# Sixteen-head attention: the value product in four passes with both halves of v in one stationary tile, its parts summed off TensorE, and the next rows normalized one slot earlier

## The reference

```
def _attention(x, W_qkv, W_out, b_out):
    qkv = x @ W_qkv                                   # 256 -> 3 x 1024
    q, k, v = jnp.split(qkv, 3, axis=-1)              # 16 heads of 64 each
    attn = jnp.einsum('bqhd,bkhd->bhqk', q, k) * DH ** (-0.5)
    attn = jax.nn.softmax(attn, axis=-1)
    out = jnp.einsum('bhqk,bkhd->bqhd', attn, v).reshape(Bq, Tq, INNER)
    return out @ W_out + b_out
x = x + g_msa * _attention(_modulate(_layernorm(x), sh_msa, sc_msa), W_qkv, W_out, b_out)
```

## Time and profile before

| | |
|---|---|
| median of 3 runs (1896.93 to 1900.22) | 1899.54 us |
| the profiled execution: its time, its span | 1899.73 us, 1897.6 us |
| share of the span busy: PE, PEld, DVE, ACT, POOL | 92%, 84%, 71%, 60%, 46% |
| granted TensorE clock, mean | 0.966 |
| the sixteen-head attention | about 262 to 1120 us |
| TensorE, idle before an instruction of the attention, from 300 to 1100 us | 27.7 us |

### The profile page before, as it was taken

One profiled execution on the slowest core, in us unless ns is written; L12 is line 12 of the kernel. 1 busy time (PEld: TensorE's weight loads), 2 busy tenths in 40 slices (PEclk: granted clock), 3 DMA queues, 4 the chain that ended last, 5 costly groups with the idle time before them and its releaser, 6 DMA issues.

```text
span 1897.6 us, 36653 instructions
## 1 busy us (share of the span) xinstructions
PE 1754.8 (92%) x12739; PEld 1587.3 (84%) x12739; DVE 1355.4 (71%) x3357; ACT 1146.9 (60%) x2858; POOL 873.6 (46%) x949
## 2 busy tenths in 40 slices
PE   5888979999999999999999979999888989989998
PEld 3657878888889888888889979999777978879997
DVE  5878866676777767677677665555999969985663
ACT  3445646666666666666666655556655746656664
POOL 1535645655665555656565533332444523331111
PEclk7999989999999999999999989999999989989999
DMA  8222200000000000000000001110111112220111
GB/s 288 64 56 70 87 20 4 10 10 10 10 10 10 9 8 10 4 10 10 10 10 10 7 15 31 29 30 27 47 43 50 52 25 44 46 58 23 45 45 45
DMA packets 110969, 65.87 MB, mean 35 GB/s; under 512 B 81530, under 2 KB 92788, under 8 KB 110788
## 3 DMA queue, kind: packets, MB, share of 16 engines
q1 hardware_dynamic: 110788, 63.54, 12.3%
HBM read 59.06 MB, written 4.46 MB: 33 GB/s over the span
## 4 chain that ended last, share of the span: by engine, by line
PE 77%; DVE 10%; issue 6%; ACT 5%; POOL 1%; DMA 1%; DVEq 0%; POOLq 0%; SPq 0%; ACTq 0%
PE bank L255 21%; PE bank L257 20%; PE bank L256 20%; PE bank L1036 7%; PE bank L985 6%; PE bank L379 2%; DVE xn L342 2%; DVE hl L577 1%; PE bank L438 1%; ACT nf L392 1%; DVE nTlo L399 1%; DVE aTlo L399 1%; ACT nThi L392 1%; ACT prob L1008 1%; DVE upd L608 1%
## 5 line engine op out<-in xcount | busy, mean ns | idle before, releaser
L1023 POOL TENSOR_SCALAR prob<-prob,rinv 128x256 f32<-128x256 f32 x512 | 467.3, 925 | 343.0 <-DVE rinv L1017 342.1
L571 ACT ACTIVATE hf<-bank,vecs 128x512 f32<-128x512 f32 x240 | 168.0, 700 | 302.4 <-PE bank L257 302.4
L577 DVE TENSOR_TENSOR hl<-hf,hh 128x512 fp32r<-128x512 f32 x240 | 196.7, 820 | 157.4 <-ACT hh L571 157.0
L1045 ACT ACTIVATE pthi<-bank 128x512 fp32r<-128x512 f32 x272 | 164.6, 605 | 196.5 <-PE bank L1036 193.9
L1008 ACT ACTIVATE prob<-bank,nmax 128x256 f32<-128x256 f32 x544 | 253.8, 479 | 39.6 <-DVE nmax L1281 21.1
L998 DVE TENSOR_REDUCE nmax<-bank 128x2 f32<-128x512 f32 x256 | 175.6, 686 | 142.1 <-PE bank L985 141.8
L334 POOL TENSOR_TENSOR rstd<-vareps,mhalf 128x2 f32<-128x2 f32 x128 | 106.1, 829 | 343.9 <-DVE vareps L330 343.2
L257 PE MATMUL bank<-WBhi,hh 128*128 128x256 f32 x768 | 217.7, 284 | 0.0
L256 PE MATMUL bank<-WBlo,hh 128*128 128x256 f32 x768 | 217.6, 283 | 0.0
L255 PE MATMUL bank<-WBhi,hl 128*128 128x256 f32 x768 | 217.3, 283 | 0.0
L255 PE MATMUL bank<-aThi,WAlo 128*128 128x256 f32 x576 | 177.4, 308 | 41.1 <-DVE aTlo L399 31.7
(11 more groups left out here) (164 smaller groups left out, 5310.6 us busy)
## 6 DMA issues: line engine op xcount, KB each, us to landing
gates<-gate_scratch SPq DMA_DIRECT2D x96, 256.0 KB, 3.7
agate<-gate_scratch SPq DMA_DIRECT2D x32, 256.0 KB, 3.2
stage<-in_L_cond_W SPq DMA_DIRECT2D x64, 64.0 KB, 2.3
out<-x SPq DMA_DIRECT2D x16, 256.0 KB, 2.2
adaw<-in_L_cond_Wc SPq DMA_DIRECT2D x1, 3072.0 KB, 17.9
stage<-in_L_cond_W_qkv SPq DMA_DIRECT2D x8, 384.0 KB, 3.5
x<-in_x SPq DMA_DIRECT2D x1, 2560.0 KB, 16.8
stage<-in_L_cond_ff_w SPq DMA_DIRECT2D x32, 64.0 KB, 2.1
```

Source lines behind the costliest of these rows:

```text
L571: last = act.activation(dst[:, :], U_BANKS[c % 2][:, :], ACTF[p], bias=vecs[:, at:at + 1])
L577: dve.tensor_tensor(hl[r][:, :], hf[r][:, :], hh[r][:, :].bitcast(F32), ALU.subtract).then_inc(h_lo, 1)
L1023: last = pool.tensor_scalar(dst[:, q, :], dst[:, q, :], rinv[i][:, q:q + 1], None, ALU.mult)
L1045: act.activation(pt[i][0][:, :], PTB[i][:, :], ACT.Copy).then_inc(pt_hi, 1)
```

## The change

Each head now has 128 columns of one tile `vv`: an even head its 64 rounded columns and then its 64 low ones, an odd head its low ones first. One pass with that stationary tile gives both products at once, the one with the rounded half in 64 partitions and the one with the low half in the other 64. Four passes a head are left (two blocks of keys, each with the low and the rounded half of the probabilities), and every head has its own 256 columns of OB. The zeros and their memsets go. The sum of the two parts is now made by other engines: ScalarE copies the low part of each head into the partitions of the main part (`oc`, two instructions a pair), VectorE adds (`of`, two instructions a pair, `o_add`) and rounds (`o_round`), and GpSimd makes the remainder (`o_rest`). TensorE's next pair waits for the two additions (`o_sum`). The copies of v from PSUM are one instruction for two. The next rows' transposes are issued in slot 9 for slot 10, the first two of their four ScalarE instructions in slot 9, the others in slot 10 ahead of the exponential, and their normalization by VectorE in slot 6 for slot 8.

```diff
-        VP = 3 * DH
-        vv = [sb(f"v{k}", [P, TPB, PAIRS * VP], F32R, att) for k in ("hi", "lo")]
+        VP = 4 * DH
+        vv = sb("vv", [P, TPB, PAIRS * VP], F32R, att)
+        of = [sb(f"of{i}", [P, SEQ], scope=att) for i in range(2)]
+        oc = sb("oc", [P, SEQ], scope=att)
...
             if h % 2 == 0 and H:
-                pe.wait_ge(o_lo, H // 2)
-            i, at = h // 2 % 2, h // 2 * VP + h % 2 * DH
+                pe.wait_ge(o_sum, H)
             for c in range(TPB):
-                last = split3(pe, OB[:, i * SEQ:(i + 1) * SEQ], [m[:, c, at:at + P] for m in vv],
-                              [m[:, c * SEQ:(c + 1) * SEQ] for m in pt[h % 2]],
-                              c == 0 and h % 2 == 0, c == TPB - 1 and h % 2 == 1)
+                for m in (1, 0):
+                    last = pe.matmul(OB[:, h % 2 * SEQ:(h % 2 + 1) * SEQ], vv[:, c, h * P:(h + 1) * P],
+                                     pt[h % 2][m][:, c * SEQ:(c + 1) * SEQ],
+                                     start=c == 0 and m == 1, stop=c == TPB - 1 and m == 0, skip_group_check=True)
             last.then_inc(pv_mm, 1)
 
-        def o_read(act, pair, i):
+        def o_halves(j):
+
+            main, rest = slice(j * DH, (j + 1) * DH), slice((1 - j) * DH, (2 - j) * DH)
+            return main, rest, slice(j * SEQ, (j + 1) * SEQ)
+
+        def o_read(act, pair):
 
             act.wait_ge(pv_mm, 2 * pair + 2)
+            if pair:
+                act.wait_ge(o_sum, 2 * pair)
+            for j in range(2):
+                main, rest, cols = o_halves(j)
+                act.activation(oc[main, :], OB[rest, cols], ACT.Copy).then_inc(o_corr, 1)
+
+        def o_add(dve, pair, i):
+
             if pair >= 2:
-                act.wait_ge(out_mm, pair - 1)
-            act.activation(oT[i][0][:, :], OB[:, i * SEQ:(i + 1) * SEQ], ACT.Copy).then_inc(o_hi, 1)
-
-        def o_rest(dve, pair, i):
-
-            dve.wait_ge(o_hi, pair + 1)
-            dve.tensor_tensor(oT[i][1][:, :], OB[:, i * SEQ:(i + 1) * SEQ], oT[i][0][:, :].bitcast(F32),
-                              ALU.subtract).then_inc(o_lo, 1)
+                dve.wait_ge(o_lo, pair - 1)
+            for j in range(2):
+                main, _, cols = o_halves(j)
+                dve.wait_ge(o_corr, 2 * pair + 2)
+                dve.tensor_tensor(of[i][main, :], OB[main, cols], oc[main, :], ALU.add).then_inc(o_sum, 1)
+
+        def o_round(dve, pair, i):
+
+            dve.wait_ge(o_sum, 2 * pair + 2)
+            if pair >= 2:
+                dve.wait_ge(out_mm, pair - 1)
+            dve.tensor_copy(oT[i][0][:, :], of[i][:, :]).then_inc(o_hi, 1)
+
+        def o_rest(pool, pair, i):
+
+            pool.wait_ge(o_hi, pair + 1)
+            pool.tensor_tensor(oT[i][1][:, :], of[i][:, :], oT[i][0][:, :].bitcast(F32),
+                               ALU.subtract).then_inc(o_lo, 1)
...
-                if i == LN_SLOT and not last:
+                if i == LAST_OWN and not last:
 
                     pe.wait_ge(proj_lo, item(b, LAST_OWN))
                     ln_transpose(pe, A, b + 1, 0)
...
                 pt_read(act, now[0], i % 2, 0)
+                if i == LN_SLOT and not last:
+                    ln_modulate(act, A, b + 1, 0, aT_hi, [1])
                 if ahead:
                     score_exp(act, ahead[0], SB_[i % 2], i % 2, prob[i % 2], 1.0)
-                if i == LN_SLOT and not last:
+                if i == LAST_OWN and not last:
 
                     act.wait_ge(proj_mm, item(b, LAST_OWN) + 1)
-                    ln_modulate(act, A, b + 1, 0, aT_hi)
+                    ln_modulate(act, A, b + 1, 0, aT_hi, [0])
```

More of the change, by code:

```diff
@@ L381, in ln_transpose, with ln_modulate @@
             last.then_inc(ln_tp, 1)
-        def ln_modulate(act, p, b, j, hi):
+        def ln_modulate(act, p, b, j, hi, parts=range(DC)):
             u = p * BATCH + b
@@ L389, in ln_modulate @@
                 act.wait_ge(ln_lo, u + 1 - sets(p, b))
-            for c in range(DC):
+            for c in parts:
                 for dst in (nf[j][:, c * SEQ:(c + 1) * SEQ], hi[c]):
@@ L394, in ln_modulate @@
                                           bias=mod[:, p, 1, c, bass.ds(b, 1)])
-            last.then_inc(ln_nf, 1)
+            if DC - 1 in parts:
+                last.then_inc(ln_nf, 1)
         def ln_rest(dve, p, b, j, hi, lo):
@@ L913, in owner, with v_heads @@
             return b + 1 if s > LN_SLOT else b
-        def v_heads(m, tile, half):
-            cols = m[:, tile, half * 4 * VP:(half + 1) * 4 * VP].rearrange("p (j w) -> p j w", w=VP)
-            return [cols[:, :, 0:DH], cols[:, :, 2 * DH:VP]]
+        def v_heads(tile, half):
+            cols = vv[:, tile, half * 4 * VP:(half + 1) * 4 * VP].rearrange("p (j w d) -> p j w d", w=4, d=DH)
+            return cols[:, :, 0:4:3, :], cols[:, :, 1:3, :]
         def proj_tensor(pe, b, s):
@@ L956, in proj_scalar @@
                 heads4 = src[:, :].rearrange("p (j h d) -> p j h d", h=2, d=DH)
-                for h, dst in enumerate(v_heads(vv[0], tile, half)):
-                    last = act.activation(dst, heads4[:, :, h, :], ACT.Copy)
-                last.then_inc(proj_hi, 1)
+                act.activation(v_heads(tile, half)[0], heads4, ACT.Copy).then_inc(proj_hi, 1)
         def proj_vector(dve, b, s):
@@ L971, in proj_vector @@
                 heads4 = src[:, :].rearrange("p (j h d) -> p j h d", h=2, d=DH)
-                for h, (hi, lo) in enumerate(zip(v_heads(vv[0], tile, half), v_heads(vv[1], tile, half))):
-                    last = dve.tensor_tensor(lo, heads4[:, :, h, :], hi.bitcast(F32), ALU.subtract)
-                last.then_inc(proj_lo, 1)
+                hi, lo = v_heads(tile, half)
+                dve.tensor_tensor(lo, heads4, hi.bitcast(F32), ALU.subtract).then_inc(proj_lo, 1)
         def pair_scores(pe, own, j):
@@ L1186, in mh_vector @@
                 if i % 2 and (i > 1 or not first):
-                    o_rest(dve, *mh_pair(b, i))
+                    o_add(dve, *mh_pair(b, i))
                 mh_projected("vector", dve, b, i, first, last)
-                if i == 8 and not last:
+                if i % 2 and (i > 1 or not first):
+                    o_round(dve, *mh_pair(b, i))
+                if i == 6 and not last:
                     ln_norm(dve, A, b + 1, 0)
@@ L1216, in mh_gpsimd @@
                     prob_weigh(pool, nxt[0], (i + 1) % 2, prob[(i + 1) % 2])
+                if i % 2 and (i > 1 or not first):
+                    o_rest(pool, *mh_pair(b, i))
                 if i == 5 and not last:
@@ L1224, in mh_gpsimd @@
                     head_norms("gpsimd", pool, A + 1)
+            if last:
+                o_rest(pool, PAIRS * b + 7, 1)
         def mh_sync(sp, b, first, last):
@@ L1232, in mh_start @@
             if name == "gpsimd":
-                for m in vv:
-                    pads = m[:, :, :].bitcast(F32).rearrange("p t (j w) -> p t j w", w=VP)[:, :, :, DH:2 * DH]
-                    for k in range(TPB):
-                        last = eng.memset(pads[:, k, :, :], 0.0)
-                last.then_inc(zeros, 1)
                 prob_weigh(eng, 0, 0, prob[0])
@@ L1267, in bass_cond_blocks @@
         qk1, kk1 = qk
-        vv1 = [[m[:, 0, i * ROWW:(i + 1) * ROWW] for m in vv] for i in range(2)]
+        vv1 = [[vv[:, k, i * ROWW:(i + 1) * ROWW] for k in range(2)] for i in range(2)]
         a1 = [[m[:, :, :] for m in aT],
-              [m[:, 1, 0:ROWW].rearrange("p (c r) -> p c r", c=DC) for m in vv]]
+              [vv[:, k, 2 * ROWW:3 * ROWW].rearrange("p (c r) -> p c r", c=DC) for k in range(2)]]
         def sh_max(dve, b):
```

13 lines of the change are left out of this document (6 added, 7 removed).

## The result

The changed kernel takes 1908.67 us (median of 6 runs, 1903.88 to 1909.56) against 1900.44 before (6 runs, 1896.93 to 1904.93): ratio 1.0036, 95% interval 1.002 to 1.0053. The forecast was 1861 us, with a range of 1830 to 1888. The profiled execution took 1903.88 us, the fastest of the six, with a span of 1901.9.

The account below looks back on a forecast made before the run. The prediction took TensorE, busy 92% of the span and one nearly unbroken stream in the attention, as the bound. From 1899.7 us, -61 - 31 - 12 + 65 + 1.5 = -38 gave 1861 us, range 1830 to 1888.

Parts of the forecast that it names:

- the passes: TensorE's value passes: two fewer a head over 256 heads, 512 x 0.12 = 61 us saved.
- the sum cost: Waits added by summing outside TensorE: 4.05 us a batch, 65 us in 16, plus 1.5 us for the last pair.
- Next rows, -31 and -12: Next rows ready one slot earlier: 15 x 2.08 = 31 us of wait saved, 8 x 1.5 = 12 of half clock.
- Durations: New instructions priced from other rows: ScalarE copy 0.38 us, VectorE addition 0.41, rounding 0.29, GpSimd subtraction 0.73.
- Start to start: Per pair, the second ScalarE copy starts 0.28 us after the first, the second VectorE addition 0.33 after the first.
- the 0.2 by which they were to be early: Odd slots: with idle engines VectorE's additions end at 1.65 us, 0.2 before TensorE's next values at 1.87.
- Two deadlines: TensorE needs the additions 1.87 us into the odd slot, and the next odd head's weighing at 5.04 (6.42 behind v).
- 1.4 us of projection hides everything: Slots 1 to 3 and 12 to 15, where the even slot has v: the projection leaves no added wait.
- VectorE late at slot 5, GpSimd at slots 7 and 9: VectorE 1.1 us late at slot 5; waits 0.2 and 1.9 in slots 3 to 7, GpSimd's weighing 0.5 late at 9.
- the weighing was to be late by 0.4: Slots 15 to 1: GpSimd's subtraction follows v's remainder, so its weighing is 0.4 us late.
- Slower: Rival: cross-partition copies take twice 0.38 us, giving 1938; slower once a copy exceeds about 0.58; chance 0.05, slower in all 0.07.
- absorbed waits would make it faster than forecast: Rival in the attention: only a third of the added waits (22 us) remains, giving 1819 us; chance 0.20.

Follow-up runs that it names:

- ln_only: The kernel before with only the next rows moved one slot earlier, the value passes unchanged: 1868.46 us, ratio 0.9826 to the kernel before.
- one_copy: The changed kernel with one ScalarE copy of 128x256 for the two of 64x256 (output partly wrong): 1874.56 us, ratio 0.9862 to the kernel before.
- exp_first: The changed kernel with v's copy behind the exponential and v's remainder behind the probabilities' in four odd slots: 1899.38 us, ratio 0.9985 to the kernel before.
- ln_copy2: ln_only plus a second ScalarE copy of each pair that nothing reads, in 14 of 16 batches: 1877.91 us, ratio 0.9885 to the kernel before.

## Why the prediction was wrong

The sum was -61 - 31 - 12 + 65 + 1.5, which is -37.5 and gives 1862 (the prediction rounded it to -38 and 1861). By the runs the passes were worth 36 where 61 was put in, the next rows 33 for 43, and the sum cost 77 for 66.5: 1901.4 - 36 - 33 + 77 = 1909. Step by step:

- *Next rows, -31 and -12.* Right in mechanism, a little large: -33 in `ln_only`. TensorE's wait went from 27.7 to 6.9 us, and the granted clock of the stretch 262 to 1120 us rose from 0.97 to 0.99. In the changed kernel the wait is 5.1 us and the clock 0.99 as well, but the move is worth only 20 us, since waits of the value change lie in the same slots.
- *Durations.* The medians of all four that the trace didn't have came out within about 0.01 us.
- *Start to start.* A term of each pair was too small: I let the second copy start 0.28 behind the first and the second addition 0.33, as full-width instructions do. They start 0.40 and 0.44 behind, and the next instruction doesn't overlap either. The Trainium skill, VectorE: DVE Perf Modes, section "Two Vector instructions with no wait between them", has this as a rule: an instruction whose input or output starts in another group of 32 partitions than the last one that read or wrote the same memory begins only when all earlier ones are finished. The trace agrees: additions at partition 0 and then 64, and full-width after them, never overlap, with or without increments. The prediction should have weighed it. Put into the prediction's steps, it makes the sums 0.12 + 0.11 us later in each pair. In the slots with v that alone takes up the 0.2 by which they were to be early; the values there start 0.24 late.
- *Two deadlines.* This is the step that failed first of all. I listed the additions and the transposes as what TensorE waits for, and wrote of the slots with v: "1.4 us of projection hides everything". There is a third deadline, the scores at the start of each even slot, which wait for the exponentials of the odd slot before. Nothing that is in the even slot can hide it. ScalarE's queue in an odd slot with v was full already: begin plus 0.20, copy, v, probabilities, exponentials, end 2.53 into the slot, and the scores at 2.68. So of the 0.24 us that two passes free there nothing could be had, and the 0.53 of the second copy came on top, less about 0.05 that one copy of v for two saves: 3.15 us for 2.68. Only the even slot gave back its 0.24, which makes the pair 7.14 for 6.90. Shown from three sides: without the second copy, -0.54 in those pairs (`one_copy`); with the exponential first, -0.4 and the wait gone (`exp_first`); with a second copy in the old kernel, +0.26 in exactly those slots (`ln_copy2`).
- *VectorE late at slot 5, GpSimd at slots 7 and 9.* Right in part. That slot 5 lasted 3.15 us for a forecast of 3.2 is luck: its values started 0.46 us late for the 0.75 priced (549.62 - 547.29 = 2.33 into the slot for 1.87), and what ended it was the wait of the scores, as in slots 3, 13 and 15 (the exponential's end 550.30, the scores 550.44). Its transposes did not wait at all. At slots 7 and 9 the transposes waited for GpSimd as forecast. Slots 4 to 7 together took 13.04 us for 13.56. Slots 8 and 9 were 0.44 longer than forecast, 10 and 11 0.5. In slot 7 the wait of GpSimd for the cast of the weights (0.30) stood at nothing in the prediction. In slots 0 and 1 the weighing was to be late by 0.4; there the transposes of slot 1 don't wait, and the values wait 0.41 for the additions, so that the 5.67 for 5.44 has another cause. That GpSimd's own subtraction is what holds was wrong for most of these slots: with it on VectorE the cast of the weights came later, the transposes of slots 1 and 5 waited for prob too, and the kernel was slower. What holds is the whole path of VectorE's queue, the cast or the reciprocal, and GpSimd's weighing.
- *The rivals.* "Slower" had 0.07 and was for another mechanism, twice the duration of a copy. It had the right engine, but the two copies cost only 0.15 us more than the 0.66 put in (0.81), where I called it slower from 0.40 more (0.58 each), and I looked only at what they do to the sums. The other side, that absorbed waits would make it faster than forecast, had 0.20 and did not occur.

Added up by slots, 16 x (53.1 - 50.3) = 45 us of the 48 that lie between 1861 and 1908.7 are found.

## What to carry to other kernels

Where one engine is busy without a gap, ask of every wait in its program how late its releaser was, not only of the waits that show idle time: a second engine can be done at the same moment, and then, as in the odd slots with v here, work taken from the first is worth nothing and work added to the second counts in full. The waits are in the instruction listing; the slack is the releaser's end against the start of the waiting row. Moving a sum off the busiest engine has to be priced by the queue of the engine that gets it, instruction by instruction to the next thing that the busiest engine needs from it. And when a change has two halves, try each alone: here one was worth 33 us and the other cost 27 to 40.

## What was not expected of the hardware

In these runs ScalarE behaves as the rule cited above says of VectorE: two copies of 64 partitions, the first written to partitions 0 to 63 and the second to 64 to 127, take 0.77 to 0.79 us together, and the next full-width instruction starts when they are over, while two full-width copies start 0.28 us apart. Increments make 0.02 us of it. That it is the change of partitions was not tried by itself (two copies on the same half), so this cause is argued from what is left. A duration of half the partitions is that of all of them: 0.380 us for 64x256 and 0.38 for 128x256.
